# Three more DRAINs on GpSimd in a kernel of attention, feed-forward and experts

## The reference

```
def _L1_ffn_ref(hidden_states, gate_w, w1, w2, w3):
    ...
    x = hidden_states.reshape(-1, Hd)
    scores = x @ gate_w.T
    mult, sel = _masked_sampling_omp(scores)
    h = jax.nn.silu(jnp.einsum('th,efh->etf', x, w1)) * jnp.einsum('th,efh->etf', x, w3)
    y = jnp.einsum('etf,ehf->eth', h, w2)
    coef = (jax.nn.one_hot(sel, gate_w.shape[0], dtype=x.dtype) * mult[..., None]).sum(axis=1)
    out = jnp.einsum('te,eth->th', coef, y)
...
x = x + jnp.tanh(g_xattn[0]) * _L0_xattn_ref(ctx_512, _layernorm(x, axis=-1), ...)
x = x + jnp.tanh(g_ffn[0]) * _L0_ffn_ref(_layernorm(x, axis=-1), ...)
x = x + jnp.tanh(g_xattn[1]) * _L1_xattn_ref(ctx_512, _layernorm(x, axis=-1), ...)
x = x + jnp.tanh(g_ffn[1]) * _L1_ffn_ref(_layernorm(x, axis=-1), ...)
return x
```

## Time and profile before

| | |
|---|---|
| median of 3 runs | 220.32 us (219.25 to 220.54) |
| profiled execution, its own time | 220.97 us |
| its span, from the first to the last instruction | 218.9 us |
| TensorE (PE) busy | 93% of the span |
| VectorE (DVE) busy | 61% |
| ScalarE (ACT), GpSimd (POOL) busy | 39% each |

### The profile page before, as it was taken

One profiled execution on the slowest core, in us unless ns is written; L12 is line 12 of the kernel. 1 busy time (PEld: TensorE's weight loads), 2 busy tenths in 40 slices (PEclk: granted clock), 3 DMA queues, 4 the chain that ended last, 5 costly groups with the idle time before them and its releaser, 6 DMA issues.

```text
span 218.9 us, 3823 instructions
## 1 busy us (share of the span) xinstructions
PE 202.9 (93%) x1282; PEld 158.8 (73%) x1282; DVE 134.5 (61%) x461; ACT 85.6 (39%) x188; POOL 85.8 (39%) x107
## 2 busy tenths in 40 slices
PE   8999979999999998998989999999999999999920
PEld 7787854435785346787979998999973599999910
DVE  4598697999988969997888495853317601111200
ACT  2678661998200646034343263222226322222100
POOL 8175316620001020054640343543877556443222
PEclk9999999999999999999999999999999999999985
DMA  5748418129999125817142221322332311022322
GB/s 170 199 192 250 114 40 260 53 70 371 413 420 417 42 68 188 315 50 237 41 139 101 27 25 24 49 41 44 66 71 26 71 13 9 7 24 27 43 25 23
DMA packets 16795, 26.07 MB, mean 119 GB/s; under 512 B 4094, under 2 KB 12421, under 8 KB 16774
## 3 DMA queue, kind: packets, MB, share of 16 engines
q1 hardware_dynamic: 11328, 20.14, 25.5%
q0 software_dynamic: 4064, 5.25, 13.7%
q10 hardware_dynamic: 1382, 0.41, 1.0%
HBM read 21.34 MB, written 5.51 MB: 123 GB/s over the span
## 4 chain that ended last, share of the span: by engine, by line
PE 35%; DVE 29%; DMA 14%; issue 9%; ACT 7%; POOL 3%; DVEq 1%; POOLq 0%; ACTq 0%
PE PS L2081 13%; DMA out_dram<-a,ids_late 9%; PE PS L2113 6%; DMA out_dram<-zb,sidx 4%; PE PS L1784 3%; PE PS L2124 3%; DVE stat L1070 3%; DVE hT L1462 3%; ACT a L841 2%; PE PS L1848 2%; DVE work L1148 2%; DVE x L1322 1%; DVE mv L1077 1%; PE PS L1835 1%; DVE work L1134 1%
## 5 line engine op out<-in xcount | busy, mean ns | idle before, releaser
L2081 PE MATMUL PS<-hT,e 128*128 128x128 f32 x512 | 62.0, 276 | 1.1 <-ACT hT L970 1.1
L2081 PEld LDWEIGHTS PS<-hT,e 128*128 128x128 f32 x512 | 60.1, 192 | 2.9 <-ACT hT L970 1.9
L1966 PE MATMUL PS<-xnT,e 128*128 128x512 f32 x88 | 39.6, 598 | 1.9 <-DVE hT L1462 1.1
L1966 PEld LDWEIGHTS PS<-xnT,e 128*128 128x128 f32 x88 | 16.1, 190 | 22.1 <-issue 17.4
L1718 DVE TENSOR_TENSOR hT<-th,PS 128x512 f32<-128x512 f32 x15 | 10.3, 687 | 35.4 <-PE PS L2081 29.3
L2113 PE MATMUL PS<-e,hT 128*128 128x256 f32 x128 | 30.6, 382 | 0.2 <-DVE x L1500 0.2
L2113 PEld LDWEIGHTS PS<-e,hT 128*128 128x128 f32 x128 | 23.1, 190 | 2.8 <-issue 0.3
L646 POOL TENSOR_TENSOR rstd<-veps,nhalf 128x2 f32<-128x2 f32 x12 | 8.7, 726 | 39.7 <-DVE veps L1079 39.6
L709 POOL DMA_INDIRECT out_dram<-a,ids_early x8 | 12.9, 1607 | 24.4 <-ACT a L1004 11.4
L1980 PE MATMUL PS<-e,hT 128*128 128x256 f32 x96 | 21.7, 383 | 0.0
L1980 PEld LDWEIGHTS PS<-e,hT 128*128 128x128 f32 x96 | 17.9, 190 | 2.9 <-issue 0.5
(11 more groups left out here) (301 smaller groups left out, 318.5 us busy)
## 6 DMA issues: line engine op xcount, KB each, us to landing
e<-e_in SPq DMA_DIRECT2D x24, 512.0 KB, 8.7
x<-x_in SPq DMA_DIRECT2D x2, 512.0 KB, 6.4
graph_rows<-e SPq DMA_DIRECT2D x4, 256.0 KB, 2.1
out_dram<-x SPq DMA_DIRECT2D x4, 256.0 KB, 2.5
xn_rows<-xn SPq DMA_DIRECT2D x4, 256.0 KB, 2.4
e<-gw_in SPq DMA_DIRECT2D x1, 768.0 KB
e<-uw_in SPq DMA_DIRECT2D x1, 640.0 KB
e<-dw_in SPq DMA_DIRECT2D x1, 640.0 KB
```

What stands on the lines that cost most here:

```text
L1966: mm = pe.matmul(PS[:, bank, :], w[:, k, it * P:(it + 1) * P], xnT[:, h, k, :], start=(k == 0), stop=(k == 1))
L2081: mm = pe.matmul(PS[:, bank + q, f * P:(f + 1) * P], w[:, k * F + f * P:k * F + (f + 1) * P], xgT[x_at][:, k, :], start=(k == 0), stop=(k ...
```

## The change

Three DRAINs are added on GpSimd. One ("retire",) ends POOL_ORDER, so it stands behind the gathers of the blocks 14 and 15 and ahead of the loop. Two stand among the late scatters, behind j = STATIC - 5 = 11 and j = STATIC - 2 = 14, the second and the fifth of the six. No other instruction is added, removed or moved on any engine. Behind the first there are then 12 indirect DMAs since L754 on GpSimd's queue; between it and the next 8; between that and the last 3; and 1 behind it.

```
--- before
+++ after
@@ -468,7 +468,7 @@
                       ("scatter", 0), ("scatter", 1), ("scatter", 2), ("scatter", 3), ("gather", 8), ("scatter", 4), ("gather", 9),
                       ("scatter", 5), ("gather_over", 0), ("gather_over", 1), ("retire",), ("scatter", 6), ("gather", 10), ("gather", 11), ("scatter", 7),
                       ("gather", 12), ("gather", 13), ("scatter", 8), ("gather_over", 2), ("gather_over", 3), ("scatter", 9),
-                      ("gather", 14), ("gather", 15)]
+                      ("gather", 14), ("gather", 15), ("retire",)]
 
         order = lambda steps, names: {step: n for n, step in enumerate(s for s in steps if s[0] in names)}
         LN = order(DVE_ORDER, ("norm_var", "attn_stats", "moe_stats"))
@@ -771,6 +771,8 @@
                     scatter_over(q, 1)
             for j in range(AT, STATIC):
                 scatter(j)
+                if j in (STATIC - 5, STATIC - 2):
+                    pool.drain()
             for q in range(2):
                 pool.wait_ge(over_gathered[q], pairs * 16 + 32)
 
```

## The result

| | before | after |
|---|---|---|
| median | 219.67 us (6 runs, 219.25 to 220.54) | 221.94 us (6 runs, 221.63 to 223.15) |
| span of the profiled execution | 218.9 us | 219.7 us |
| GpSimd busy | 85.8 us | 84.8 us |

The ratio is 1.0094, with a 95% interval of 1.007 to 1.0118: slower by 2.1 us (the medians lie 2.3 us apart).

What follows compares the result with a forecast made beforehand. The prediction took GpSimd's chain of scatters behind 175.99 us to bound the end. Its terms, 1.7 + 0.8 + 0.7 - 0.45 = 2.75 us, took the median from 220.32 to 223.0 us, range 221.2 to 224.9.

Steps and rivals of the forecast that it cites:

- Rival B: At the DRAINs, wait past landing grows with past transfers: 0.6 + 0.5 + 0.3 + 0.2 = 1.6 us, 221.9 us; chance 0.25.
- What bounds the end: Behind 175.99 us, a chain of scatters: every microsecond GpSimd's queue is held adds to the end; TensorE and ScalarE aren't late.
- The law of x: At GpSimd's DRAINs, x is the further time after its transfers land; estimates 0.8, 0.7, 0.6 and 0.6 us.
- the list: At GpSimd's DRAINs, the reading that x walks past transfers: 0.17 + 0.036 us per transfer.
- the fixed time: At GpSimd's DRAINs, the reading that x is 1.05 us whatever came before; as a rival 224.5 us, chance 0.28.
- The DRAIN ahead of the loop: Behind the last gathers: it makes the loop's first scatter late by 0.9 + x, a cost of 1.7 us.
- copies 1.2 us: Between the DRAIN ahead of the loop and its first scatter: three small index copies, taken as 1.2 us.
- The two in the tail: DRAINs among the late scatters: the landing wait is free, each costs x + 0.1, so 0.8 and 0.7 us.
- The DRAIN at the end: At the program's end: one transfer left where it had 24, x from 1.05 to 0.6, a gain of 0.45 us.
- The flight of a scatter: Issue to landing of a late scatter, 3.7 to 3.8 us; a change behind a DRAIN would make the prediction wrong altogether.
- Rival C: The tail's DRAINs finish their walk during the flight; x is 0.17 at all four places, cost 0.7 us, 221.0 us; chance 0.08.
- Rival D: The added DRAINs do nothing on the path, costing a few ns each: 220.3 us; chance 0.02.

Runs made afterwards that it cites:

- no_retire: The kernel before without its own DRAIN at L754, so 50 indirect DMAs lie ahead of the last DRAIN; ratio 1.0034, 0.75 us slower.
- load_first: The kernel before with one DRAIN more ahead of the loop, behind the read of the number of pairs; ratio 1.0001.
- after_again: The changed kernel measured again without edits, against the kernel before; ratio 1.0043, 0.9 us.
- fetch_moved2: The changed kernel with 36 more TensorE instructions, met semaphore waits spread over twelve places, to move its instruction fetch; 221.12 us, ratio 1.0076 against the kernel before.
- tail_only: The kernel before with only the two DRAINs among the late scatters added, none ahead of the loop; ratio 1.0039, 0.9 us.

## Why the prediction came out as it did

I forecast 223.0 us from a median of 220.32, a loss of 2.7 us, and 2.1 us were measured (1.5 to 2.6 by the interval). The time, 221.94, lies in the range of 221.2 to 224.9. That it lies there is luck. The terms that I named come to 0.6 us (point 5), which would be 220.9 us and under the range. The rest is mostly a pause and a long landing that I had not foreseen, 0.35 and 1.0 us in the profile. The second series of the same kernel, 220.79 us, is under the range. Rival B's 221.9 is as close by the same luck.

1. *What bounds the end.* Right. Every delay behind zb went into the time, and TensorE and ScalarE left the chain. Their distance is small at one place, though: in no_retire scatter 11 is issued at 195.40, 0.1 us behind its operand from ScalarE (194.82 + 0.48), and the chain runs through TensorE up to there.
2. *The law of x.* I took values halfway between the list and the fixed time, and it is the list: rival B, which I gave 0.25. 0.036 per transfer was the slope there, 0.041 is measured over 1 to 50. What I held against it, 0.8 us at L754, came from taking 2.8 us for a gather's landing. That one landed after 2.5 us, and x is 1.10.
3. *The DRAIN ahead of the loop*, forecast 1.7 us, was 0.6. The step that failed is the term "copies 1.2 us". It took three copies in 0.4 us (174.04 to 174.48), where the rows of before had them at 1.4 and 0.9 us. Those stood right behind the descriptors of an indirect DMA. Here GpSimd had been idle for 3.43 us, and the last copy took 0.18 us. VectorE is not what makes the difference: in the second pass of the kernel after, with VectorE idle since 179.75, the copies behind the scatter's descriptors took 0.80 and 0.67 us again (180.41 and 180.66). The rest of the difference is x, 0.53 in place of 0.8; the restart of the sequencer took 1.1 us, as forecast. load_first shows the mechanism: with the register load ahead of the DRAIN nothing is late.
4. *The two in the tail*, forecast 0.8 and 0.7 us, were 0.85 and 0.3. The first holds 0.38 of x, 0.1 of registers and 0.35 of the pause, which I did not foresee. Without the pause it would have been 0.5.
5. *The DRAIN at the end*, forecast a gain of 0.45 us, gave 0.8. The sum of list prices with the quick copies is 0.6 + 0.5 + 0.3 - 0.8 = 0.6 us. The pause makes it 0.9 us, which is near what after_again measured (0.9 us by its ratio, 0.8 by the medians), although its profiled run has the long landing too; eight of its twelve runs lie under 221.3.
6. *The flight of a scatter*, of which I said that I would be wrong if it changed. It did, by 0.8 to 1.4 us in the three profiles. That this is what lifts two of the series to 1.0079 and 1.0094 is likely and not shown: fetch_moved2, without it, measured 1.0076.

Rival C, cover, was wrong in its mechanism: the flight doesn't hide all of the walk, and x is 0.38 and 0.53 us where C has 0.17. Its 0.7 us are near the 0.6 of the list prices, and far from the 2.1 measured. Rival D fell with every DRAIN read.

## What to carry to other kernels

In this kernel a DRAIN on GpSimd costs by the indirect DMAs since the last one, 0.04 us each behind the last landing, and the one at the program's end pays for all that are left. Put one where the engine is early and see that no register load or other start-up of the sequencer stands behind it: one such place halved the bill at the end, 2.10 to 1.03 us, and the times show 0.75 us of gain, while DRAINs in a chain of transfers only pay it earlier. Where a chain of short transfers sets the end, one instruction more can cost 0.35 us by where the sequencer's pause falls, so a change of under a microsecond should be judged with the pauses read off the chain.

## What the runs showed of the hardware

- The DRAIN with everything landed took 2.03 us for 24 indirect DMAs, and 46 ns right behind another. I had expected 1.0 us.
- A 16 KB instruction fetch of one engine delayed another engine's scatter by 0.8 to 1.4 us where packets of the scatter were left to run behind it (three profiles), and by nothing where none was (tail_only).
- In a gap of 2.9 us TensorE's granted clock fell from 1.00 (29 to 30 us) to 0.50 (31 to 32 us), its lower level of 1.2 GHz. It was 0.50 still from 36 to 40 us, with TensorE busy all the time, and 1.00 again from 41 us on. The 35 instructions that did it, met waits all, cost some 6 us ahead of zb.
- Three small copies of indices took 1.4 us in all right behind an indirect DMA's descriptors and 0.4 us when GpSimd had been idle before them.
- The Trainium skill, VectorE: DVE Perf Modes, section "The DRAIN you can't avoid", has start and end DRAINs at about 12 ns on all five engines. SP's 7 ns agrees. At the end of the kernel before, VectorE's took 457 ns, ScalarE's 504 and TensorE's 1310. On GpSimd those at the end took 3.7 to 5.8 us behind indirect DMAs here, and the one at the start 174 ns; only the one right behind another DRAIN came near, at 46 ns. The measurement decides, and here it disagrees.
